# One scatter of whole rows per tile, two under way within an expert, in the routed experts of the second layer

## The chip, the cores and the metric

The kernel runs on one NeuronCore of one Trainium2 chip. The metric is the device time of one launch in microseconds, here the median of three runs. The core has a tensor engine (PE, with its weight loads shown apart as PEld), a vector engine (DVE), a scalar engine (ACT), GpSimd (POOL) and a sync engine (SP), and sixteen DMA engines that all of these feed.

## The reference, cut to what matters

The program computes two layers on `x`, 4 x 512 = 2048 tokens of 512 floats; each layer adds an attention-like block and then a mixture of experts to the residual. The change touches only the very last block, the mixture of experts of the second layer (layer 1):

```python
E, G, TKG, K = (32, 8, 4, 8)
I, SI = (256, 512)
...
_, top_k_index = jax.lax.top_k(masked, K)
tkw = jnp.take_along_axis(scores, top_k_index, axis=-1)
...
flat_idx = top_k_index.reshape(-1)
sort_idx = jnp.argsort(flat_idx)
xs = jnp.repeat(x, K, axis=0)[sort_idx]
group_sizes = jnp.bincount(flat_idx, length=E).astype(jnp.int32)
gate = jax.lax.ragged_dot(xs, w_gate, group_sizes)
up = jax.lax.ragged_dot(xs, w_up, group_sizes)
down = jax.lax.ragged_dot(jax.nn.silu(gate) * up, w_down, group_sizes)
unsort = jnp.argsort(sort_idx)
routed = (down[unsort].reshape(T, K, H) * tkw[..., None]).sum(axis=1)
shared = jax.nn.silu(x @ sw_gate) * (x @ sw_up) @ sw_down
return (routed + shared).reshape(hidden_states.shape)
```

Each of the 2048 tokens goes to 8 different experts of 32. Each expert is a gated two-matmul block with inner width 256, and the eight weighted results of a token are summed onto its row.

## The kernel before, in words

The program runs stage after stage. The last two matter here. The router stage of layer 1 (lines 700 to 1240) computes the shared expert, picks the experts of each token, and writes the token rows, sorted by expert, into a buffer `slots_in` of 128-row tiles. Each expert's rows are padded up to a multiple of 128, so that a tile belongs to one expert; `NTILE1` = 159 tiles are always worked, the last ones being padding alone. The same stage writes the residual with the shared expert's result into the output `out`, and zeros into 128 spare rows behind it (line 838). A list `expert` says which expert each tile has.

The last stage is `expert_stage1` (line 1775). It adds every tile's result to the output rows of its tokens. Tile `t` passes through the engines like this:

- ACT loads rows of four tiles at a time (`load_rows`, L1898) into `xs`, and their records, that is, weights, slot numbers and token number, into `rec` (L1903).
- DVE transposes the rows in `turned_rows` (L1950), and PE multiplies with gate and up weights in `up` (L2012). ACT takes the SiLU (L1886), DVE the product (L1960).
- PE transposes the hidden values (L2019), DVE copies them out (L1955), and PE multiplies with the down weights in `down` (L2028), one tile behind `up`. PE reads the expert of a tile from `ids` with `value_load` (L2005, L2023).
- ACT scales the result by the routing weight and puts it into one of eight buffers `yo` (`empty`, L1893). It waits there for `added`, which says that the scatter of the tile eight before is done with the buffer.
- DVE works out the addresses in `addressed` (L1969 to L1978). It waits for `added` in the same way. A padding row gets a spare row as its address.
- POOL scatters the tile onto the output with an accumulating indirect DMA (`add`, L1865). The output is viewed as half rows of 256 floats, so each tile takes two scatters of 128 half rows. Each half column has a semaphore of its own (`half_out`), and the scatter of a half waits until the same half of the tile before has landed, because two tiles of different experts may hold the same token. So at most two scatters are under way, the two halves of about one tile, and tiles follow each other strictly.

SP refills the ring of four experts' weights (`refill`, L1839 to L1843), each time that `down` has passed the last tile of an expert. `hold` is a wait with a small semaphore increment behind it (L73 and L74). The loop on POOL is unrolled by eight tiles (`OUT`), and the first and last turns are written out. No planner sets the order; each engine runs its list, and semaphores join them.

Of the kernel before, what the change touches and what calls it, by code (L numbers as in the profile page):

```python
# [14 lines left out]
F32 = mybir.dt.float32  # L15
BF16 = mybir.dt.bfloat16
I32 = mybir.dt.int32
ALU = mybir.AluOpType
# [3 lines left out]
P = 128  # L22
B, S, H = 4, 512, 512
T = B * S
NT = T // P
# [13 lines left out]
F1, FS1, K1 = 256, 512, 8  # L39
# [3 lines left out]
NTILE1 = (T * K1 + E * (P - 1)) // P  # L43
# [651 lines left out]
def route_stage(nc, c, I, D, x, L, route, ahead=None, out=None):  # L695
# [10 lines left out]
    with ExitStack() as ctx:  # L706
        pl = Pools(nc, ctx)
# [11 lines left out]
        h = sb("h", [P, FC, S])  # L719
# [11 lines left out]
        else:  # L731
# [4 lines left out]
            base = sb("base", [P, E])  # L736
# [11 lines left out]
        token_i = sb("token_i", [P, NT], I32)  # L748
# [38 lines left out]
        with nc.Block() as block:  # L787

            @block.sync
            def _(sp):  # L790
# [44 lines left out]
                    sp.wait_ge(sem["xout"], 1 + 16 * B)  # L835
                    sp.wait_ge(sem["ahead"], 1 + 16 * loads[0])
                else:
                    sp.dma_start(out[T:T + P, :].rearrange("p (a z) -> p a z", z=P), bc(c["zeros"][:, :], 1, H // P))\
                      .then_inc(sem["xout"], 16)
                    sp.wait_ge(sem["eid"], 1 + 1)  # L840
                    sp.dma_start(D["expert"].rearrange("(p a) o -> p (a o)", a=2), tei[:, :]).then_inc(sem["eidout"], 16)
                    for e in range(AHEAD):
# [4 lines left out]
                                     x[:, b * TB:(b + 1) * TB, :]).then_inc(sem["xout"], 16)  # L847
                    sp.wait_ge(sem["eidout"], 1 + 16)
                    sp.wait_ge(sem["ahead"], 1 + 48 * AHEAD)
                    sp.wait_ge(sem["xout"], 1 + 16 * (B + 1))  # L850

            @block.gpsimd
            def _(pool):
                pool.memset(seg[:, :, :], 1.0).then_inc(sem["ones"], 1)
                pool.memset(seg_t[:, :, :], 1.0).then_inc(sem["ones"], 1)
                if L == 1:
                    pool.memset(seg8[:, :, :], 1.0).then_inc(sem["ones"], 1)
                pool.wait_ge(sem["ones"], 1 + 2 + L)
                pool.memset(seg[:, :, 0], 0.0).then_inc(sem["seg"], 1)
                pool.memset(seg_t[:, :, 0], 0.0).then_inc(sem["seg"], 1)  # L860
                if L == 1:
                    pool.memset(seg8[:, :, 0], 0.0).then_inc(sem["seg"], 1)
                each = 1 if L == 0 else 2
                pool.iota(token_i[:, :], [[each * P, NT]], base=1, channel_multiplier=each).then_inc(sem["iota"], 1)
                for b in range(B if L == 0 else 0):
                    pool.wait_ge(sem["ve"], 1 + b + 1)
                    pool.tensor_tensor(rs[:, b % 2, :], ve[:, b % 2, :], c["minus_half"][:, 0:TB], ALU.pow).then_inc(sem["rs"], 1)

                for t in range(NT):
                    if L == 1 and t < TB:  # L870
                        pool.wait_ge(sem["idx0"], 1 + t + 1)
                    else:
                        pool.wait_ge(sem["idx"], 1 + t // TB + 1 - L)
                    for k in range(K):
# [900 lines left out]
def expert_stage1(nc, c, I, D, x, ends, W, out):  # L1775
# [3 lines left out]
    with ExitStack() as ctx:  # L1779
        pl = Pools(nc, ctx)  # L1780
# [3 lines left out]
        OUT = 2 * RING  # L1784
# [15 lines left out]
        ids = pl.sb("e1_ids", [1, NTILE1], I32)  # L1800
        slot_i = pl.sb("e1_sloti", [P, NTILE1], I32)
        slot1 = pl.sb("e1_slot1", [P, NTILE1])
        spare_i = pl.sb("e1_sparei", [P, 1], I32)
        spare1 = pl.sb("e1_spare1", [P, 1])
        mine = pl.sb("e1_mine", [P, 2, K1])
        wrow = pl.sb("e1_wrow", [P, OUT, 1])
        pad = pl.sb("e1_pad", [P, 2, 1])
        dest = pl.sb("e1_dest", [P, OUT, 2], I32)
        HC = H // 2
        halves = out.rearrange("t (a h) -> (t a) h", a=2)  # L1810
        ps_g = pl.ps("e1_psg", [P, 2, 512])
        ps_h = pl.ps("e1_psh", [P, 2, 512])
        ps_o = pl.ps("e1_pso", [P, 2, 512])
        sem = {n: pl.sem("e1_" + n) for n in ("ids", "w0", "w1", "w2", "w3", "ready", "xsT", "gu", "sg", "h",
                                              "htr", "hT", "down", "yo", "added", "preset", "iota", "named", "chosen", "first", "dest")}
        landed = [sem[f"w{s}"] for s in range(RING)]
        rows_in = [pl.sem0(f"e1_rows{r}") for r in range(2)]
        rec_in = [pl.sem0(f"e1_rec{r}") for r in range(2)]
        half_out = [pl.sem0(f"e1_out{a}") for a in range(2)]
        ROUNDS = -(-NTILE1 // RING)  # L1820
        LAST = NTILE1 - (ROUNDS - 1) * RING
        assert 1 < LAST < RING
# [5 lines left out]
        with nc.Block() as block:  # L1828
# [24 lines left out]
            @block.gpsimd  # L1853
            def _(pool):
                pool.iota(slot_i[:, :], [[P, NTILE1]], base=1, channel_multiplier=1).then_inc(sem["iota"], 1)
                pool.iota(spare_i[:, :], [[1, 1]], base=2 * T + 1, channel_multiplier=2).then_inc(sem["iota"], 1)

                def add(t, q, first=False):
                    hold(pool, sem["yo"], 1 + t + 1, c["held"])
                    for a in range(2):  # L1860
                        if not first:
                            hold(pool, half_out[a], 16 * t, c["held"])
                            if a == 1:
                                pool.sem_inc(sem["added"], 1)  # L1864
                        pool.indirect_dma_start(halves, bass.IndirectOffsetOnAxis(dest[:, q, a:a + 1], 0),  # L1865
                                                yo[:, q, a * HC:(a + 1) * HC], None,
                                                bounds_check=2 * (T + P) - 1, oob_is_err=True, compute_op=ALU.add)\
                            .then_inc(half_out[a], 16)

                add(0, 0, first=True)  # L1870
                for q in range(1, OUT):
                    add(q, q)
                with pool.Fori(1, TURNS - 1) as i:  # L1873
                    for q in range(OUT):
                        add(i * OUT + q, q)
                for t in range((TURNS - 1) * OUT, NTILE1):
                    add(t, t % OUT)
                for a in range(2):
                    pool.wait_ge(half_out[a], 16 * NTILE1)

            @block.scalar
            def _(act):
# [60 lines left out]
            def _(dve):  # L1943
# [18 lines left out]
                def addressed(t, q, n):  # L1962
                    row = rec[:, q // RING, q % RING, :]
                    if q % RING == 0:
                        dve.wait_ge(rec_in[q // RING], 16 * n)
                    if not (isinstance(t, int) and t < OUT):
                        dve.wait_ge(sem["yo"], 1 + t - OUT + 1)
                        dve.wait_ge(sem["added"], 1 + t - OUT + 1)
                    dve.scalar_tensor_tensor(out=mine[:, q % 2, :], in0=row[:, K1:2 * K1], scalar=slot1[:, bass.ds(t, 1)],  # L1969
                                             in1=row[:, 0:K1], op0=ALU.is_equal, op1=ALU.mult).then_inc(sem["named"], 1)  # L1970
                    dve.scalar_tensor_tensor(out=pad[:, q % 2, :], in0=row[:, 2 * K1:RECW], scalar=0.0, in1=spare1[:, :],
                                             op0=ALU.is_equal, op1=ALU.mult).then_inc(sem["named"], 1)
                    dve.wait_ge(sem["named"], 1 + 2 * (t + 1))
                    dve.tensor_reduce(wrow[:, q, :], mine[:, q % 2, :], AX_X, ALU.add).then_inc(sem["chosen"], 1)
                    dve.scalar_tensor_tensor(out=dest[:, q, 0:1], in0=pad[:, q % 2, :], scalar=-1.0, in1=row[:, 2 * K1:RECW],
                                             op0=ALU.add, op1=ALU.add).then_inc(sem["first"], 1)
                    dve.wait_ge(sem["first"], 1 + t + 1)
                    dve.tensor_tensor(dest[:, q, 1:2], pad[:, q % 2, :], row[:, 2 * K1:RECW], ALU.add)\  # L1978
                       .then_inc(sem["dest"], 1)

                def a_round(i, first=False, last=False):
                    for q in range(REST if last else OUT):
# [5 lines left out]
                        product(t, q)  # L1988
                        addressed(t, q, i + 1)

                dve.wait_ge(sem["iota"], 1 + 2)
                dve.tensor_copy(slot1[:, :], slot_i[:, :]).then_inc(sem["preset"], 1)
                dve.tensor_copy(spare1[:, :], spare_i[:, :]).then_inc(sem["preset"], 1)
                dve.wait_ge(sem["preset"], 1 + 2)
                turned_rows(0, 0, 1, first=True)
                a_round(0, first=True)
# [1135 lines left out]
```

## Time and profile before

| | |
|---|---|
| median of three runs | 3114.5 us |
| the three runs | 3119.78, 3114.5, 3114.5 us |
| time of the profiled execution | 3106.26 us |
| its span on the core | 3104.5 us |
| mean granted TensorE clock | 0.949 |
| PE busy | 2687.9 us (87%) |
| DVE busy | 1493.2 us (48%) |
| POOL busy | 1367.1 us (44%) |
| ACT busy | 773.7 us (25%) |
| last stage, first load to end of span | 2155.0 to 3104.5 us |

Times in the rows are counted from the start of the span. Busy shares are averages over stages of different kind. In the last stage the scatters are short instructions on POOL whose transfers run on after them, so a busy share of POOL says little about how far behind the scatters are: that is read from the start times of single instructions.

### The profile page before, as it was taken

The page shows a single profiled execution, that of the slowest core. Times are in us where ns is not written, and L with a number is a line of the kernel's source. Part 1 is how long each engine was busy: PE and PEld are TensorE (multiplying, and loading weights), DVE is VectorE, ACT ScalarE, POOL GpSimd, SP SyncE. Part 2 cuts the span into 40 slices and gives each one's busy share as a digit, 9 for nine tenths or more (in the row PEclk, how much of TensorE's full clock was granted, in tenths as well). Part 3 has the DMA queues.
Part 4 walks back from the last instruction along what each step waited for, and adds up shares of the span by engine and source line. Part 5 has one row for each costly group of instructions (what it writes and reads, how often), then busy time and mean ns, then how long its engine had stood idle before and what let it go on. Part 6 is the DMA issues. An engine that isn't in the chain of part 4 may idle for free. (4 is left out here: it accounts for less than half of the span.)

```text
span 3104.5 us, 33211 instructions
## 1 busy us (share of the span) xinstructions
PE 2687.9 (87%) x8933; PEld 1175.3 (38%) x8936; DVE 1493.2 (48%) x2766; ACT 773.7 (25%) x1190; POOL 1367.1 (44%) x960
## 2 busy tenths in 40 slices
PE   5888975799999887689999998981999999899995
PEld 2343431344444333233333334430444444444442
DVE  7999999332000232266666646310444444344442
ACT  4746653200000010133434332000121111111111
POOL 2777656143000131136646431465455555455555
PEclk8999999999999998889999999995999999999997
DMA  3334222310300599750474001555777776877664
GB/s 125 113 100 111 78 66 54 113 56 14 114 0 14 209 355 333 220 151 1 122 202 116 1 1 59 207 196 194 152 150 161 145 124 126 189 143 163 127 102 53
DMA packets 386408, 385.06 MB, mean 124 GB/s; under 512 B 72195, under 2 KB 311364, under 8 KB 386307
## 3 DMA queue, kind: packets, MB, share of 16 engines
q1 hardware_dynamic: 212434, 243.23, 25.0%
q0 software_dynamic: 68272, 97.19, 16.1%
q10 hardware_dynamic: 105600, 43.35, 6.6%
q8 instruction: 56, 0.92, 0.1%
q14 instruction: 46, 0.37, 0.0%
HBM read 236.15 MB, written 160.27 MB: 128 GB/s over the span
## 5 line engine op out<-in xcount | busy, mean ns | idle before, releaser
L1865 POOL DMA_INDIRECT out_x<-e_yo,e_dest x318 | 493.3, 1551 | 447.8 <-DMA out_x<-e_yo,e_dest 303.5
L2012 PE MATMUL e_psg<-e_wgu,e_xsT 128*128 x1272 | 578.3, 598 | 79.9 <-DVE e_xsT L1950 79.9
L285 POOL TENSOR_TENSOR hc<-hs,bcst 128x1024 f32<-128x1024 f32 x128 | 300.8, 2350 | 175.4 <-DVE ps_b L505 169.5
L2012 PEld LDWEIGHTS e_psg<-e_wgu,e_xsT 128*128 128x128 f32 x1272 | 233.1, 193 | 312.4 <-issue 312.4
L2028 PE MATMUL e_pso<-e_wd,e_hT 128*128 x636 | 306.2, 604 | 27.4 <-DVE e_hT L1955 26.7
L630 PE MATMUL ps_y<-hc,ident 128*128 128x512 f32 x512 | 242.5, 612 | 86.6 <-POOL hc L285 86.4
L511 DVE TENSOR_TENSOR_SCAN hs<-dA,ps_b 128x1024 f32<-128x1024 f32 x128 | 292.6, 2286 | 6.6 <-ACT dA L415 2.4
L1960 DVE TENSOR_TENSOR e_h<-e_psg,e_sg 128x256 f32<-128x256 f32 x159 | 67.3, 423 | 345.1 <-ACT e_sg L1886 335.3
L1233 PE MATMUL r_ps_t<-r_wd,r_h 128*128 128x512 f32 x480 | 209.6, 597 | 8.7 <-DVE r_h L982 5.1
L1886 ACT ACTIVATE e_sg<-e_psg 128x256 f32<-128x256 f32 x159 | 61.1, 384 | 543.9 <-PE e_psg L2012 538.5
L982 DVE TENSOR_TENSOR r_h<-r_ps_u,r_sg 128x512 f32<-128x512 f32 x60 | 41.4, 691 | 319.5 <-PE r_ps_u L1214 296.1
L415 ACT ACTIVATE dA<-dt,a_neg 128x511 f32<-128x511 f32 x256 | 165.4, 713 | 109.2 <-DVE hs L511 104.2
L2028 PEld LDWEIGHTS e_pso<-e_wd,e_hT 128*128 128x128 f32 x636 | 119.3, 191 | 188.5 <-issue 188.4
L2616 DVE TENSOR_REDUCE a_nm<-a_ps 128x2 f32<-128x992 f32 x128 | 146.1, 1185 | 88.9 <-PE a_ps L2860 88.5
L880 POOL DMA_INDIRECT slots_in<-r_xn,scat x128 | 126.6, 989 | 135.8 <-DMA slots_in<-r_xn,scat 60.3
L1893 ACT ACTIVATE e_yo<-e_pso,e_wrow 128x512 f32<-128x512 f32 x159 | 109.3, 687 | 288.4 <-PE e_pso L2028 217.4
L1950 DVE STREAM_TRANSPOSE e_xsT<-e_xs 128x512 f32<-128x512 f32 x159 | 174.6, 1098 | 12.8 <-DMA e_xs<-slots_in 7.3
L630 PEld LDWEIGHTS ps_y<-hc,ident 128*128 128x128 f32 x512 | 93.2, 192 | 230.7 <-POOL hc L285 135.7
L2378 ACT ACTIVATE a_pt<-a_ps 128x1024 f32<-128x1024 f32 (+1 forms) x128 | 126.2, 1022 | 184.0 <-PE a_ps L2877 123.3
L915 ACT ACTIVATE r_sg<-r_ps_g 128x512 f32<-128x512 f32 x60 | 35.8, 597 | 523.2 <-PE r_ps_g L1214 504.4
L505 DVE TENSOR_TENSOR ps_b<-du,bcst 128x1024 f32<-128x1024 f32 x128 | 159.3, 1244 | 8.3 <-DVE hs L511 0.5
L1214 PE MATMUL r_ps_g<-r_xnT,r_wgu 128*128 128x512 f32 x352 | 158.7, 593 | 0.0
(411 smaller groups left out, 3517.8 us busy)
## 6 DMA issues: line engine op xcount, KB each, us to landing
slots_in<-zeros SPq DMA_DIRECT2D x160, 256.0 KB, 2.3
e_xs<-slots_in ACTq DMA_DIRECT2D x160, 256.0 KB
bcst<-bc_rows SPq DMA_DIRECT2D x128, 256.0 KB, 4.3
e_wgu<-in_wg SPq DMA_DIRECT2D x32, 512.0 KB
e_wgu<-in_wu SPq DMA_DIRECT2D x32, 512.0 KB
e_wd<-in_wd SPq DMA_DIRECT2D x32, 512.0 KB
e_w<-in_wg SPq DMA_DIRECT2D x11, 1408.0 KB
e_w<-in_wu SPq DMA_DIRECT2D x11, 1408.0 KB
```

The lines of the kernel that those rows point to most:

```text
L285: pool.tensor_tensor(hc[:, it % 2, half(h), :], hs[:, it % 2, half(h), :], bc(bcst[:, q, 1, :], 1, HB), ALU.mult).then_inc(sem["hc"], 1)
L415: i = act.activation(dA[:, it % 2, t, 1:], dt[:, b % 2, t, 1:], ACT.Exp, scale=a_neg[:, n, t:t + 1])
L505: dve.tensor_tensor(ps_b[:, :, :], du[:, b % 2, half(h), :], bc(bcst[:, q, 0, :], 1, HB), ALU.mult)\
L511: dve.tensor_tensor_scan(hs[:, it % 2, half(h), :].rearrange(flat), dA[:, it % 2, half(h), :].rearrange(flat), ps_b[:, :, :].rearrange(fla ...
L630: i = pe.matmul(ps_y[:, t, :], c["ident"][:, :], hc[:, it % 2, t, :], start=False, stop=False, skip_group_check=True)
L1214: i = pe.matmul(ps[:, f % 2, :], w[:, k, f * P:(f + 1) * P], xnT[:, b, k, :], start=k == 0, stop=k == KH - 1)
L1233: i = pe.matmul(ps_t[:, j % 2, :], h[:, f, j * P:(j + 1) * P], wd[:, f, :], start=f == 0, stop=f == FC - 1)
L1865: pool.indirect_dma_start(halves, bass.IndirectOffsetOnAxis(dest[:, q, a:a + 1], 0), yo[:, q, a * HC:(a + 1) * HC], None, bounds_check=2 * ...
L1950: dve.transpose(xsT[:, q % 2, :, :].rearrange("p k (s j) -> p k s j", j=DQ), xs[:, q // RING % 2, part, :].rearrange("p s (i k) -> p k s i ...
L2012: j = pe.matmul(ps_g[:, q % 2, :], xsT[:, q % 2, k, :], wgu[:, bass.ds(e % RING, 1), k, :], start=k == 0, stop=k == KH - 1)
L2028: j = pe.matmul(ps_o[:, q % 2, :], hT[:, q % 2, a, :], wd[:, bass.ds(e % RING, 1), a, :], start=a == 0, stop=a == NW - 1)
L2616: dve.tensor_reduce(nm[:, i % 8, 2 * z:2 * z + 2], ps[:, at:at + 2, 0:S2], AX_X, ALU.max, negate=True)\
```

## The change

The view of the output as half rows goes. Each tile is scattered with one instruction of 128 whole rows of 512 floats, 2 KB each. Semaphores now go by the parity of the tile (`out_of[0]` for even tiles, `out_of[1]` for odd ones). The scatter of tile `t` always waits for the one of tile `t - 2`. It waits for the one of tile `t - 1` only if that tile has another expert; tiles of one expert share no token, except padding, and padding rows now go to one of two sets of 128 spare rows by parity. Which count of the other parity to wait for stands in a small table `after`, worked out once by DVE from `ids`; POOL reads its entry with `value_load` before each scatter, except for the first three tiles. `added` is now raised when POOL comes to tile `t + 2` and no longer at `t + 1`. DVE loses one small operation per tile (L1978) and the wait ahead of it. The output has 256 spare rows instead of 128, so the router stage writes zeros with two transfers.

```diff
-                    sp.dma_start(out[T:T + P, :].rearrange("p (a z) -> p a z", z=P), bc(c["zeros"][:, :], 1, H // P))\
-                      .then_inc(sem["xout"], 16)
+                    for a in range(2):
+                        sp.dma_start(out[T + a * P:T + (a + 1) * P, :].rearrange("p (a z) -> p a z", z=P),
+                                     bc(c["zeros"][:, :], 1, H // P)).then_inc(sem["xout"], 16)
...
-                each = 1 if L == 0 else 2
-                pool.iota(token_i[:, :], [[each * P, NT]], base=1, channel_multiplier=each).then_inc(sem["iota"], 1)
+                pool.iota(token_i[:, :], [[P, NT]], base=1, channel_multiplier=1).then_inc(sem["iota"], 1)
...
-                pool.iota(spare_i[:, :], [[1, 1]], base=2 * T + 1, channel_multiplier=2).then_inc(sem["iota"], 1)
-
-                def add(t, q, first=False):
+                pool.iota(spare_i[:, :], [[P, 2]], base=T + 1, channel_multiplier=1).then_inc(sem["iota"], 1)
+                pool.iota(after_i[:, :], [[16, (NTILE1 + 1) // 2], [16, 2]], base=-16, channel_multiplier=0).then_inc(sem["iota"], 1)
+                pool.wait_ge(sem["after"], 1 + 1)
+
+                def add(t, q, turn):
+
+                    same = 8 * OUT * turn + 16 * (q // 2)
+                    head = isinstance(turn, int) and turn == 0
                     hold(pool, sem["yo"], 1 + t + 1, c["held"])
-                    for a in range(2):
-                        if not first:
-                            hold(pool, half_out[a], 16 * t, c["held"])
-                            if a == 1:
-                                pool.sem_inc(sem["added"], 1)
-                        pool.indirect_dma_start(halves, bass.IndirectOffsetOnAxis(dest[:, q, a:a + 1], 0),
-                                                yo[:, q, a * HC:(a + 1) * HC], None,
-                                                bounds_check=2 * (T + P) - 1, oob_is_err=True, compute_op=ALU.add)\
-                            .then_inc(half_out[a], 16)
+                    if head and q < 3:
+                        before = 16 if q > 0 else None
+                    else:
+                        before = pool.value_load(after[0:1, bass.ds(t, 1)], min_val=16, max_val=16 * NTILE1)
+                    if before is not None:
+                        hold(pool, out_of[1 - q % 2], before, c["held"])
+                    if not (head and q < 2):
+                        hold(pool, out_of[q % 2], same, c["held"])
+                        pool.sem_inc(sem["added"], 1)
+                    pool.indirect_dma_start(out[:, :], bass.IndirectOffsetOnAxis(dest[:, q, 0:1], 0), yo[:, q, :], None,
+                                            bounds_check=T + 2 * P - 1, oob_is_err=True, compute_op=ALU.add)\
+                        .then_inc(out_of[q % 2], 16)
...
                     dve.scalar_tensor_tensor(out=dest[:, q, 0:1], in0=pad[:, q % 2, :], scalar=-1.0, in1=row[:, 2 * K1:RECW],
-                                             op0=ALU.add, op1=ALU.add).then_inc(sem["first"], 1)
-                    dve.wait_ge(sem["first"], 1 + t + 1)
-                    dve.tensor_tensor(dest[:, q, 1:2], pad[:, q % 2, :], row[:, 2 * K1:RECW], ALU.add)\
-                       .then_inc(sem["dest"], 1)
+                                             op0=ALU.add, op1=ALU.add).then_inc(sem["dest"], 1)
...
+                dve.wait_ge(sem["ids"], 1 + 16)
+                dve.tensor_tensor(apart[:, 1:], ids[:, 1:], ids[:, 0:NTILE1 - 1], ALU.not_equal).then_inc(sem["apart"], 1)
+                dve.wait_ge(sem["apart"], 1 + 1)
+                dve.scalar_tensor_tensor(out=after[:, 1:], in0=apart[:, 1:], scalar=16.0, in1=after_i[:, 1:NTILE1],
+                                         op0=ALU.mult, op1=ALU.add).then_inc(sem["after"], 1)
```

## Rows read from the trace of the kernel before

**Rows 1.** The page: tenths busy per slice; the chain that ended last.
```profile
PE   5888975799999887689999998981999999899995
POOL 2777656143000131136646431465455555455555
PEclk8999999999999998889999999995999999999997
DMA out_x<-e_yo,e_dest 20%; PE e_psg L2012 3%; PE e_pso L2028 1%; POOL out_x L1865 1%; DMA e_xs<-slots_in 0%; POOLq L73 0%; PE e_psh L2019 0%; POOLq L1865 0%; POOLq L74 0%; ACT e_yo L1893 0%; DVE e_xsT L1950 0%; POOLq L1864 0%; ACTq L1898 0%; POOLq L1873 0%; DVE e_hT L1955 0%
```
**Rows 2.** Timeline, ACT's L1893: start, duration, instruction, idle time before and its releaser.
```profile
2177.39 0.69 ACT L1893 ACTIVATE e_yo<-e_pso,e_wrow 128x512 f32<-128x512 f32 x1 [1.33 <-PE e_pso L2028]
2424.77 0.69 ACT L1893 ACTIVATE e_yo<-e_pso,e_wrow 128x512 f32<-128x512 f32 x1 [1.33 <-PE e_pso L2028]
2440.15 0.69 ACT L1893 ACTIVATE e_yo<-e_pso,e_wrow 128x512 f32<-128x512 f32 x1 [5.82 <-DVE e_dest L1978]
3065.75 0.69 ACT L1893 ACTIVATE e_yo<-e_pso,e_wrow 128x512 f32<-128x512 f32 x1 [1.33 <-PE e_pso L2028]
3068.62 0.69 ACT L1893 ACTIVATE e_yo<-e_pso,e_wrow 128x512 f32<-128x512 f32 x1 [2.18 <-PE e_pso L2028]
```
**Rows 3.** Timeline, POOL's L1865.
```profile
2178.99 1.62 POOL L1865 DMA_INDIRECT out_x<-e_yo,e_dest  x1 [23.64 <-ACT e_yo L1893]
3087.97 1.55 POOL L1865 DMA_INDIRECT out_x<-e_yo,e_dest  x1 [0.86 <-DMA out_x<-e_yo,e_dest]
3092.57 1.55 POOL L1865 DMA_INDIRECT out_x<-e_yo,e_dest  x1 [0.93 <-DMA out_x<-e_yo,e_dest]
3094.84 1.55 POOL L1865 DMA_INDIRECT out_x<-e_yo,e_dest  x1 [0.72 <-issue]
```
**Rows 4.** Two stretches: length, busy time of each engine, granted clock, DMA share.
```profile
2177.39:2424.77 247.38, 247.38 (x646) 115.65 (x645) 108.86 (x363) 49.30 (x93) 125.71 (x81) 1.00 0.77 158
2424.77:3065.75 640.98, 611.83 (x1556) 279.75 (x1554) 272.65 (x892) 118.93 (x222) 346.61 (x224) 0.99 0.71 134
```
**Rows 5.** Waits from 1750 us on: in total, times, longest.
```profile
POOL out_x L1865 <- DMA out_x<-e_yo,e_dest: 303.5, 148, 5.7
DVE e_mine L1969 <- POOLq L1864: 138.8, 74, 4.9
PE e_pso L2028 <- DVE e_hT L1955: 26.7, 19, 2.7
```
**Rows 6.** The chain, two stretches: start, duration, what.
```profile
2696.95 8.40 DMA out_x<-e_yo,e_dest
...
3087.97 3.75 DMA out_x<-e_yo,e_dest
...
3091.85 0.72 issue
```
**Rows 7.** The end of the stage (line 1828): duration in ns, first and last start.
```profile
L1828 POOLq DRAIN  x1: 4842/4842/4842, 3098.8 to 3098.8; - x1
```
**Rows 8.** Layer 0's scatter of whole rows (line 1437): ns min/median/max; landing.
```profile
L1437 POOL DMA_INDIRECT x_after<-e_yo,e_dest x16: 1534/1556/2469, 1073.3 to 1271.7; - x16
DMA to landing us min/median/max: 4.9/8.6/10.2
```
**Rows 9.** DMA queue of POOL, 3070 to 3097 us (12 issues): packets, MB, share.
```profile
q0 software_dynamic: 1611, 1.46, 49.3%
```
**Rows 10.** DMA queues of POOL and SP, 1070 to 1280 us.
```profile
q1 hardware_dynamic: 19213, 59.87, 82.3%
q0 software_dynamic: 2304, 4.20, 11.5%
```
**Rows 11.** PE's queue at line 2023: ns min/median/max.
```profile
L2023 PEldq FUSED_REGOPS  x197: 46/151/156, 2172.6 to 3065.3; - x197
L2023 PEldq TENSOR_LOAD <-e_ids x159: 296/302/825, 2172.3 to 3064.9; - x159
```
**Rows 12.** Groups of instructions: busy us, mean ns, idle before.
```profile
L1978 DVE TENSOR_TENSOR e_dest<-e_pad,e_rec 128x1 int32<-128x1 f32 x159 | 28.7, 181 | 5.5
```
**Rows 13.** Timeline of the stage's start.
```profile
2154.97 0.31 SPq L1832 DMA_DIRECT2D e_ids<-tile_expert  x1
...
2155.38 0.24 DVE L1992 CAST e_slot<-e_sloti 128x159 f32<-128x159 int32 x1 [65.94 <-POOL e_sparei L1856]
...
2162.96 2.05 DVE L1950 STREAM_TRANSPOSE e_xsT<-e_xs 128x512 f32<-128x512 f32 x2 [7.28 <-DMA e_xs<-slots_in]
```
**Rows 14.** Waits of SP from 2170 us on.
```profile
SPq L74 <- PE e_pso L2028: 554.2, 25, 48.4
SPq L74 <- DMA e_wd<-in_wd: 5.4, 1, 5.4
```

More of the change, by code:

```diff
@@ L849, in _ @@
                     sp.wait_ge(sem["ahead"], 1 + 48 * AHEAD)
-                    sp.wait_ge(sem["xout"], 1 + 16 * (B + 1))
+                    sp.wait_ge(sem["xout"], 1 + 16 * (B + 2))
             @block.gpsimd
@@ L1802, in expert_stage1 @@
         slot1 = pl.sb("e1_slot1", [P, NTILE1])
-        spare_i = pl.sb("e1_sparei", [P, 1], I32)
-        spare1 = pl.sb("e1_spare1", [P, 1])
+        spare_i = pl.sb("e1_sparei", [P, 2], I32)
+        spare1 = pl.sb("e1_spare1", [P, 2])
+        apart = pl.sb("e1_apart", [1, NTILE1], I32)
+        after_i = pl.sb("e1_afteri", [1, NTILE1 + 1], I32)
+        after = pl.sb("e1_after", [1, NTILE1], I32)
         mine = pl.sb("e1_mine", [P, 2, K1])
@@ L1807, in expert_stage1 @@
         pad = pl.sb("e1_pad", [P, 2, 1])
-        dest = pl.sb("e1_dest", [P, OUT, 2], I32)
-        HC = H // 2
-        halves = out.rearrange("t (a h) -> (t a) h", a=2)
+        dest = pl.sb("e1_dest", [P, OUT, 1], I32)
         ps_g = pl.ps("e1_psg", [P, 2, 512])
@@ L1814, in expert_stage1 @@
         sem = {n: pl.sem("e1_" + n) for n in ("ids", "w0", "w1", "w2", "w3", "ready", "xsT", "gu", "sg", "h",
-                                              "htr", "hT", "down", "yo", "added", "preset", "iota", "named", "chosen", "first", "dest")}
+                                              "htr", "hT", "down", "yo", "added", "preset", "iota", "named", "chosen", "dest",
+                                              "apart", "after")}
         landed = [sem[f"w{s}"] for s in range(RING)]
@@ L1818, in expert_stage1 @@
         rec_in = [pl.sem0(f"e1_rec{r}") for r in range(2)]
-        half_out = [pl.sem0(f"e1_out{a}") for a in range(2)]
+        out_of = [pl.sem0(f"e1_out{lane}") for lane in range(2)]
+        assert NTILE1 % 2 == 1 and OUT % 2 == 0
         ROUNDS = -(-NTILE1 // RING)
@@ L1870, in _ @@
-                add(0, 0, first=True)
-                for q in range(1, OUT):
-                    add(q, q)
+                pool.iota(spare_i[:, :], [[P, 2]], base=T + 1, channel_multiplier=1).then_inc(sem["iota"], 1)
[4 more added lines that the diff above has]
+                    head = isinstance(turn, int) and turn == 0
+                    hold(pool, sem["yo"], 1 + t + 1, c["held"])
+                    if head and q < 3:
[10 more added lines that the diff above has]
+                        .then_inc(out_of[q % 2], 16)
@@ L1873, in _ @@
+                for q in range(OUT):
+                    add(q, q, 0)
                 with pool.Fori(1, TURNS - 1) as i:
                     for q in range(OUT):
[L1875 to L1879, printed above, removed]
+                        add(i * OUT + q, q, i)
+                for q in range(REST):
+                    add((TURNS - 1) * OUT + q, q, TURNS - 1)
@@ L1881, in _ @@
+                pool.wait_ge(out_of[0], 16 * (NTILE1 // 2 + 1))
+                pool.wait_ge(out_of[1], 16 * (NTILE1 // 2))
             @block.scalar
@@ L1970, in addressed @@
                                              in1=row[:, 0:K1], op0=ALU.is_equal, op1=ALU.mult).then_inc(sem["named"], 1)
-                    dve.scalar_tensor_tensor(out=pad[:, q % 2, :], in0=row[:, 2 * K1:RECW], scalar=0.0, in1=spare1[:, :],
-                                             op0=ALU.is_equal, op1=ALU.mult).then_inc(sem["named"], 1)
+                    dve.scalar_tensor_tensor(out=pad[:, q % 2, :], in0=row[:, 2 * K1:RECW], scalar=0.0,
+                                             in1=spare1[:, q % 2:q % 2 + 1], op0=ALU.is_equal, op1=ALU.mult)\
+                       .then_inc(sem["named"], 1)
                     dve.wait_ge(sem["named"], 1 + 2 * (t + 1))
@@ L1989, in a_round @@
                         addressed(t, q, i + 1)
-                dve.wait_ge(sem["iota"], 1 + 2)
+                dve.wait_ge(sem["iota"], 1 + 3)
                 dve.tensor_copy(slot1[:, :], slot_i[:, :]).then_inc(sem["preset"], 1)
                 dve.tensor_copy(spare1[:, :], spare_i[:, :]).then_inc(sem["preset"], 1)
+                dve.wait_ge(sem["ids"], 1 + 16)
[3 more added lines that the diff above has]
+                                         op0=ALU.mult, op1=ALU.add).then_inc(sem["after"], 1)
                 dve.wait_ge(sem["preset"], 1 + 2)
@@ L3127 @@
          for k, v in host.items()}
-    out = nc.dram_tensor("out_x", (T + P, H), F32, kind="ExternalOutput").ap()
+    out = nc.dram_tensor("out_x", (T + 2 * P, H), F32, kind="ExternalOutput").ap()
     program(nc, I, out)
```

## The prediction

> **What bounds the kernel now.** I began with the slices of the page [rows 1]. From about the 28th slice on PE is near full and POOL half busy, which looks like a stage that PE bounds. The chain of waits of the same page says otherwise: what ended last is one run of scatter transfers, 20% of the span, with PE hardly in it. So I looked at when each tile is put into its `yo` buffer by ACT and when POOL scatters it, tile by tile in the timeline.
>
> Tile 0 goes into its buffer at 2177.39 us, tile 46 at 2424.77, tile 157 at 3065.75, the last one at 3068.62 [rows 2]. The first 46 steps take 247.38 us, 5.378 us each, and PE is busy without a gap and at full clock in them [rows 4]. The 111 steps from tile 46 to 157 take 640.98 us, 5.775 each. In this stretch PE has 29.2 us of idle time (640.98 less 611.83), and a clock of 0.99. What holds it back is in the waits [rows 5]: PE waits for DVE's copy, 26.7 us, but DVE itself sits in the address operation until POOL raises `added`, 138.8 us over 74 times. Tile 48, for instance, enters its buffer only after ACT has waited 5.82 us for an address [rows 2]. The eight buffers are full from there on, and PE runs at POOL's pace.
>
> POOL issues the first scatter at 2178.99 us, 1.6 us after the buffer began to be filled, and the last tile's at 3092.57 and 3094.84 [rows 3]. That is 158 tiles in 913.6 us, 5.78 us per tile, and POOL never catches up: at the end it is 24 to 26 us behind ACT. Its idle time is spent on its own transfers, 303.5 us [rows 5]. Calm, a tile takes 4.60 us (3087.97 to 3092.57) [rows 3], for two instructions of 1.55 us and their overhead. A half lands 3.75 us after its issue when it is calm and up to 8.40 us after it under load [rows 6]. So the bound of the stage is the order of the scatters, in two forms: PE's lost pace and the tail.
>
> **The change part by part.** Terms that lie on the path:
>
> 1. PE's lost pace. If POOL keeps up, the 111 steps go at 5.378 us: 596.9 instead of 641.0, a gain of 44.1 us. 29.2 of it is the idle time shown; the rest is the lower clock and slower steps behind each gap. The first stretch is good evidence that nothing else is next in line, since loads of rows and weights and all scatters went on in it, with a DMA share of 0.77 against 0.71 later [rows 4]. SP waited for weights once, for 5.4 us, and otherwise for PE [rows 14], so weights are ahead.
>
> 2. The tail. Today the last issue is 26.2 us behind ACT (3094.84 less 3068.62) [rows 2, 3]. If POOL keeps up it is 1.6 us plus the new read of `after`. PE does such a read in 0.30 us, with 0.15 us of register work behind it [rows 11]. That makes 2.1 us: a gain of 24.1 us.
>
> 3. The last landing. Twelve half scatters took 49.3% of sixteen engines for 27 us, 1.11 us of all engines each [rows 9]. The sixteen whole-row scatters of layer 0 took 11.5% of 210 us, 1.51 us each [rows 10]. So a whole row costs 0.4 us more per landing (and 0.7 us less than two halves). The only whole-row landings in the trace took 4.9 us at best [rows 8], 1.15 more than 3.75. I take 0.8, between the two. The 5.9 us from the last landing (3094.84 + 3.75) to the end of the span, with the drain of 4.84 us in it [rows 7], stay.
>
> Whether POOL keeps up is the real question. Its own time per tile: one instruction, 1.556 us for whole rows in layer 0 [rows 8], so as long as a half's; 0.72 us ahead of it [rows 6]; 0.45 for the read; the waits, some 0.4. That is 3.1 us, against 5.378 that PE leaves. Bounds for the read are nothing (if it runs ahead under the instruction before) and 0.98 us (the longest load of rows 11 and its register work); both stay under. Then the landings. The mean step of today's chain, landing and what follows it to the next issue, is 5.78 us, since POOL is nearly always behind; with 0.4 us more it is 6.2. In an expert of five tiles, tiles 1, 3 and 5 each wait for a landing, and 2 and 4 go beside them. The next expert waits for tile 5. Three steps for five tiles is 3.7 us per tile, and an expert of four takes two steps and 3.1 us, 3.9 per tile. There are 32 experts, so at most 31 changes in 158 neighbours, and the mean is five tiles. At a change POOL falls 6.2 less 5.4, 0.8 us, behind and makes it up on the next tile. Under load one landing may be 9 us; the buffers hold that. `added` comes a tile later than before, which leaves six or seven useful buffers instead of seven or eight; that costs nothing while POOL is one or two tiles behind, and about 5 us of cover if it is not. I add 2 us for some lag left at the end.
>
> Edits at no cost: DVE loses an operation of 0.18 us per tile [rows 12], but PE is full in the first stretch with it, so it gives nothing. The table `after` needs `ids`, loaded from 2154.97 on; DVE idles for 7.28 us until the first rows have landed at 2162.96 [rows 13], which covers a wait for `ids`, two small operations and the third iota. If `ids` came after the rows, some 0.5 us would go. The second transfer of zeros is issued early in the router stage and ends long before the stage does; its cover gone, it would cost a microsecond. The wait for `after` on POOL has nothing behind it until 2178.99 [rows 3].
>
> The sum: 44.1 + 24.1 - 0.8 - 2 = 65.4 us. From 3106.3 (span 3104.5 and 1.8 around it) the profiled execution comes to 3040.9. The median of the runs is 8.2 us above the profiled execution, so the time is 3114.5 - 65.4 = 3049 us.
>
> Two rules weighed. The trace shows 0.3 us for a register read on PE's queue [rows 11]. By the Trainium skill, DMA: Bandwidth & Descriptors, Latency and other measured facts, such a load has a floor of about 600 ns; by it the sum would be 0.3 us less, since only the last tile's read is bare. The trace disagrees for PE, and none of its rows shows a read on POOL. The calm halves landed after 3.75 us [rows 6], with 1.55 us of instruction in it. The same page, Anatomy of one DMA, puts a transfer at 2.0 us fixed and bytes over 436 GB/s, an estimate of 0.3 us more for 256 KB than for 128; the engine time of accumulating rows here gives 0.4, and by the rule the sum would be larger by 0.5 us.
>
> **The rivals.** A, the forecast: POOL keeps up, 3049 us.
>
> B, the landing grows. The one place with whole-row scatters had landings of 8.6 us in the median [rows 8]. With a step of 9.5 us, three steps for five tiles are 5.7 us per tile: 158 tiles end at 2179 + 901 = 3080, then a landing of 4.6 and 5.9 us of end, 3090.5, a gain of 14 us: 3100. For it: two transfers of 256 KB are in flight now. Against it: there SP's queue took 82.3% of the DMA engines [rows 10], while the whole share here is 0.71 to 0.77 [rows 4] with gaps in it, and the scatters' part of that shrinks.
>
> C, slower: pairs don't overlap. If the waits let only one whole-row scatter go at a time, or the second transfer queues behind the first until it has landed, the step of 6.2 us holds for every tile. POOL then issues the last one at 2179 + 158 x 6.2 = 3158.6, and the span ends at 3169, 64.6 us later than now: 3179. It decides from a mean pace of 5.79 us per tile on, where the gain is gone. Against it: halves of one tile overlap on the same queue today, as two issues 2.27 us apart at the end with landings of 3.75 show [rows 3, 6].
>
> D, only the tail goes. If another wait held PE as much in the second stretch, 24.1 - 2.8 = 21 us are won: 3093. The gapless first 46 tiles speak against it.
>
> **How the numbers follow.** A 0.80, with an own range of 3040 to 3062 (the profiled run's offset of 8 us, a lag of up to 10 us). B 0.08, D 0.06, C 0.06. The range reaches towards B and D: 3038 to 3082. What a measurement here can tell from no change is about 0.2%, 6 us; the three runs spread by 5.3. A, most of B and D are faster: 0.91. Same takes 0.03, from between B and C, slower 0.06.
>
> **What would show it.** ACT's L1893 should step at 5.38 us to the end, with the last at 3025 us, and DVE's wait for `added` should be gone. PE should have no gap over 0.3 us in the stage and a clock of 1.00. 159 scatters of about 1.56 us, the last issued 2 to 6 us after ACT's last start. Landings of 4.2 to 9 us. POOL's idle time should be put down to ACT, not to its DMA. The forecast is wrong if POOL is over four tiles behind for long (B), if no scatter is issued while another of its expert is under way (C), or if PE has gaps with another releaser (D).

## The result, and the profile after

The changed kernel takes 3040.64 us in the median of four runs (3035.01 to 3042.43), against 3114.69 us for four runs of the kernel before (3114.5 to 3119.78). The ratio is 0.9764, with a 95% interval of 0.9744 to 0.9784. The forecast was 3049 us and a gain of 65 us; by the medians the gain is 74 us. The profiled executions are 3106.26 and 3042.43 us, with spans of 3104.5 and 3040.7 us, so between them it is 63.8 us.

The page of the changed kernel answers to [rows 1]: first two lines of its slices (tenths busy), then the start of its chain (shares of the span by engine, then by line).

```profile
PE   5888975799999887588999998994499999999998
POOL 2777656233100041126555632257322222232222
...
PE 27%; DMA 1%; issue 0%; POOL 0%; SPq 0%; DVE 0%; ACTq 0%; POOLq 0%; ACT 0%; DVEq 0%
PE e_psg L2025 17%; PE e_pso L2041 9%; PE e_psh L2032 1%; DMA out_x<-e_yo,e_dest 1%; DMA e_xs<-slots_in 0%; POOL out_x L1877 0%; ACTq L1908 0%; SPq L1769 0%; DVE e_xsT L1960 0%; POOLq L1871 0%; ACT e_yo L1903 0%; SPq L1771 0%; DVE e_h L1970 0%; ACT e_sg L1896 0%; POOLq L74 0%
```

The chain has changed hands. Before, scatter transfers held 20% of the span; now PE's matmuls hold 27% and the scatters 1%. POOL's share in the last stage is halved, and PE has no slice below full after the first of the stage, but for the last, in which the span ends.

The timeline of ACT, filling the buffers (start, duration, instruction, idle time before it with its releaser), for tiles 0, 46, 157 and 158:

```profile
2179.00 0.69 ACT L1903 ACTIVATE e_yo<-e_pso,e_wrow 128x512 f32<-128x512 f32 x1 [1.33 <-PE e_pso L2041]
2426.38 0.69 ACT L1903 ACTIVATE e_yo<-e_pso,e_wrow 128x512 f32<-128x512 f32 x1 [1.33 <-PE e_pso L2041]
3025.96 0.69 ACT L1903 ACTIVATE e_yo<-e_pso,e_wrow 128x512 f32<-128x512 f32 x1 [1.33 <-PE e_pso L2041]
3028.83 0.69 ACT L1903 ACTIVATE e_yo<-e_pso,e_wrow 128x512 f32<-128x512 f32 x1 [2.18 <-PE e_pso L2041]
```

The first 46 steps take 247.38 us, to the hundredth what they took before [rows 2]. The next 111 take 599.58 us instead of 640.98, 5.40 us each. The stretches behind this, as in [rows 4]:

```profile
2179.00:2426.38 247.38, 247.38 (x646) 115.65 (x645) 101.50 (x323) 49.30 (x93) 71.43 (x46) 1.00 0.80 163
2426.38:3025.96 599.58, 597.26 (x1556) 279.06 (x1554) 244.84 (x776) 118.87 (x222) 172.11 (x111) 1.00 0.74 143
```

PE is idle for 2.3 us in the second stretch, not 29.2, and its granted clock is 1.00. That is one gap, and the kernel before had it too, with 2.36 us. It is a wait for SP. The chain around it (start, duration, what):

```profile
2845.91 0.58 SPq L1769
2846.54 0.62 SPq L1769
2847.20 0.65 SPq L1771
...
2848.10 0.02 SPq L1839
2848.12 0.48 PE e_psh L2032 x2
```

SP had waited 12.6 us for PE's `down`. Released by it at 2845.84 us, it first issued three loads of a later expert's weights, and only then raised `ready` (L1839), which tells PE that the next expert's weights are there. SP's wait for their landing shows no idle time, so they lay ready. The gap comes from the order of SP's list, not from a late load.

POOL's scatters at the start and the end of the stage, as in [rows 3]:

```profile
2180.59 1.63 POOL L1877 DMA_INDIRECT out_x<-e_yo,e_dest  x1 [23.60 <-ACT e_yo L1903]
2186.68 1.58 POOL L1877 DMA_INDIRECT out_x<-e_yo,e_dest  x1 [4.45 <-ACT e_yo L1903]
2196.91 1.55 POOL L1877 DMA_INDIRECT out_x<-e_yo,e_dest  x1 [8.65 <-issue]
2198.76 1.55 POOL L1877 DMA_INDIRECT out_x<-e_yo,e_dest  x1 [0.30 <-issue]
...
3022.96 1.55 POOL L1877 DMA_INDIRECT out_x<-e_yo,e_dest  x1 [3.84 <-DMA out_x<-e_yo,e_dest]
3028.33 1.57 POOL L1877 DMA_INDIRECT out_x<-e_yo,e_dest  x1 [3.82 <-DMA out_x<-e_yo,e_dest]
3031.20 1.56 POOL L1877 DMA_INDIRECT out_x<-e_yo,e_dest  x1 [1.30 <-issue]
```

The third line is a tile that waited for a landing under load, and the fourth goes out 1.85 us behind it while the third is still under way. The last issue is 2.4 us behind ACT's last start; before, it was 26.2 us.

One row is a trap. The profile puts most of POOL's idle time down to its own transfers, as it did before [rows 5]:

```profile
POOL out_x L1877 <- DMA out_x<-e_yo,e_dest: 343.6, 94, 4.7
POOL out_x L1877 <- issue: 212.6, 57, 9.1
POOL out_x L1877 <- ACT e_yo L1903: 72.9, 8, 23.6
```

Near the end of the stage this is not so. The chain there has landings of 4.75 us, and the issue at 3028.33 us is followed by one at 3031.20, 2.87 us later, with the first still on its way. The 2.87 us is ACT's own step from tile 157 to 158. So POOL waits for ACT there, and the landing only happens to come at about the same time.

### The profile page after: what moved, and what is told of

It is laid out like the page before. It is cut to its first block and busy times, and to the rows that moved or that the text cites. A ratio compares the mean times of both kernels' runs of the same rounds, so it can differ in the third digit from the quotient of the medians.

```text
span 3040.7 us, 33280 instructions
## 1 busy us (share of the span) xinstructions
PE 2672.1 (88%) x8935; PEld 1175.4 (39%) x8936; DVE 1459.8 (48%) x2609; ACT 773.9 (25%) x1190; POOL 1121.2 (37%) x803
## 5 line engine op out<-in xcount | busy, mean ns | idle before, releaser
L1877 POOL DMA_INDIRECT out_x<-e_yo,e_dest x159 | 246.7, 1551 | 629.1 <-DMA out_x<-e_yo,e_dest 343.6
L2041 PE MATMUL e_pso<-e_wd,e_hT 128*128 x636 | 298.9, 592 | 0.7 <-ACT e_yo L1903 0.7
L982 DVE TENSOR_TENSOR r_h<-r_ps_u,r_sg 128x512 f32<-128x512 f32 x60 | 41.4, 691 | 318.1 <-PE r_ps_u L1214 308.8
```

The lines of the kernel that those rows point to most:

```text
L1877: pool.indirect_dma_start(out[:, :], bass.IndirectOffsetOnAxis(dest[:, q, 0:1], 0), yo[:, q, :], None, bounds_check=T + 2 * P - 1, oob_is_ ...
L2041: j = pe.matmul(ps_o[:, q % 2, :], hT[:, q % 2, a, :], wd[:, bass.ds(e % RING, 1), a, :], start=a == 0, stop=a == NW - 1)
```

## The experiments

Every ratio is against the kernel before, which took 3103 to 3122 us beside these runs (medians 3113.2, 3109.5 and 3109.6). The edits are made to the changed kernel, where the text names no other.

**Whole rows alone.** The table `after` is filled as if no neighbour had the same expert.

```diff
-dve.tensor_tensor(apart[:, 1:], ids[:, 1:], ids[:, 0:NTILE1 - 1], ALU.not_equal)
+dve.tensor_tensor(apart[:, 1:], ids[:, 1:], ids[:, 1:], ALU.is_equal)
```

> Whole rows as in the change, but the table is filled as if every tile had another expert than the one before, so each scatter waits for all earlier ones. Order theory (the waits between scatters set the stage): the step of each tile is one whole-row landing, 5.6 us in the mean of the changed kernel's trace, and some 1.0 us to the next issue, 6.6 us; 158 steps put the span's end near 3235 us, slower than before by 60 to 130 us, and POOL is 30 us and more behind ACT. Packet theory (half as many packets and half as many instructions on POOL make the gain, the overlap is a bystander): the time stays near the changed kernel's, below 3070 us.

Measured: 3214.73 us, ratio 1.0337 (1.0312 to 1.0362). Whole rows without the overlap are 102 us slower than the kernel before, inside the 60 to 130 us of the order theory. POOL's first and last issue are at 2178.47 and 3203.18 us, 6.49 us per tile (1024.7 over 158). In the calm end of the stage a tile takes 5.8 us. First the timeline of POOL, then the waits of DVE, which stands for PE's lost pace:

```profile
3191.58 1.55 POOL L1877 DMA_INDIRECT out_x<-e_yo,e_dest  x1 [4.36 <-issue]
3197.41 1.57 POOL L1877 DMA_INDIRECT out_x<-e_yo,e_dest  x1 [4.28 <-issue]
3203.18 1.56 POOL L1877 DMA_INDIRECT out_x<-e_yo,e_dest  x1 [4.20 <-issue]
```

```profile
DVE e_mine L1979 <- POOLq L1876: 447.3, 132, 7.4
```

In the kernel before, the same calm end has 4.60 us per tile with halves [rows 3]. The chain of this run names the landing, 4.88 us for a whole row, where a half took 3.75 [rows 6]:

```profile
3185.67 4.88 DMA out_x<-e_yo,e_dest
```

The packet theory, which expected less than 3070 us, is out.

**The overlap alone.** Two halves per tile as before, four semaphores (parity and half), and the changed kernel's rule.

```diff
-                    if before is not None:
-                        hold(pool, out_of[1 - q % 2], before, c["held"])
...
+                    for a in range(2):
+                        if before is not None:
+                            hold(pool, out_of[1 - q % 2][a], before, c["held"])
+                        if not (head and q < 2):
+                            hold(pool, out_of[q % 2][a], same, c["held"])
+                            if a == 1:
+                                pool.sem_inc(sem["added"], 1)
+                        pool.indirect_dma_start(halves, bass.IndirectOffsetOnAxis(dest[:, q, a:a + 1], 0),
+                                                yo[:, q, a * HC:(a + 1) * HC], None,
```

> Two half-row scatters per tile as before the change, but with the changed kernel's rule: a tile waits for the tile before it only if that one has another expert. Order theory: POOL's two instructions need 4.6 us per tile, under PE's 5.38, and a landing is exposed only at a change of expert, so most of the gain is there: 3045 to 3075 us, with POOL behind at experts of one to three tiles. Packet theory: no gain, 3105 to 3120 us.

Measured: 3043.67 us, ratio 0.9788 (0.9764 to 0.9811). The intervals of this and the changed kernel overlap, so in the timed runs the rule alone brings all that can be measured; the time is 1.3 us below the expected range. The traces show a little more. From ACT's first start to the end of the span it is 865.5 us here and 861.7 in the changed kernel: the last issue is 5.3 us behind ACT's last start and not 2.4, and the rest from there to the end takes 0.9 us more. So 3.8 us of the gain belong to the whole rows, at the very end. POOL is busier than before the change and it doesn't matter (length, busy time of PE, PEld, DVE, ACT and POOL, clock, DMA share, GB/s):

```profile
2200.00:2600.00 400.00, 400.00 (x1043) 187.04 (x1042) 179.81 (x599) 79.90 (x150) 232.83 (x150) 1.00 0.78 152
```

POOL's 150 instructions of this stretch take 232.8 of its 400 us, and PE is full at full clock.

**The read moved ahead of the wait.**

```diff
-                    hold(pool, sem["yo"], 1 + t + 1, c["held"])
                     if head and q < 3:
                         before = 16 if q > 0 else None
                     else:
                         before = pool.value_load(after[0:1, bass.ds(t, 1)], min_val=16, max_val=16 * NTILE1)
+                    hold(pool, sem["yo"], 1 + t + 1, c["held"])
```

> The changed kernel with POOL's read of the table moved ahead of the wait for the tile. Order theory: the read (0.29 us and 0.15 us of register work) is bare in each tile, so the last issue comes about 0.6 us sooner behind ACT (1.8 instead of 2.4 us), the time is the same within what can be measured, and the idle time that the profile puts down to the DMA goes over to ACT. If POOL truly waited for landings within an expert, the distance stays at 2.4 us and the releaser stays the DMA.

Measured: 3040.8 us (3038.13 to 3043.11), the same as the changed kernel. The last issue is at 3028.30 us, 1.8 us behind ACT's last start at 3026.48, 0.6 us closer. The expectation on the releaser was half a miss. The sum put down to the DMA fell from 343.6 to 265.1 us, but it went to "issue" (212.6 to 327.2 us), and in the steady end the profile names the DMA as before:

```profile
3025.43 1.57 POOL L1877 DMA_INDIRECT out_x<-e_yo,e_dest  x1 [3.83 <-DMA out_x<-e_yo,e_dest]
3028.30 1.56 POOL L1877 DMA_INDIRECT out_x<-e_yo,e_dest  x1 [1.30 <-issue]
```

The distance behind ACT fell by 0.55 us, about the read's time (0.29 us and 0.15 of register work), which a true wait for a landing would have swallowed. So the distance decides, and the name of the releaser doesn't.

**Overlap for even tiles only.** Odd tiles always wait for the tile before.

```diff
-                    if head and q < 3:
+                    if q % 2 == 1:
+                        before = 8 * OUT * turn + 16 * (q // 2 + 1)
+                    elif head and q < 3:
```

> The changed kernel with overlap allowed only to even tiles; odd tiles always wait for the tile before them. Order theory with a threshold: two tiles take one landing step and one bare issue, (6.6 + 3) / 2 = 4.8 us per tile, still under 5.38, so the time is the changed kernel's within 8 us. If the gain went with the share of overlapped pairs, the time would lie halfway between the changed kernel's and the serial one's.

Measured: 3039.64 us, ratio 0.9774 (0.9751 to 0.9798), nothing lost. POOL was up to 25.5 us behind ACT in the stretch of small experts, which the eight buffers took. A gain in proportion to the overlapped pairs would have ended halfway to the serial run, near 3128 us, and is out. There is a threshold, and the changed kernel is well inside it.

**Overlap for every fourth tile only.** As the last, with `if q % 2 == 1 or q % 4 == 2:` and `before = 8 * OUT * turn + 16 * ((q + 1) // 2)`.

> Overlap allowed to every fourth tile only, eight buffers. Threshold theory, from the steps measured: 6.49 us for a tile that waits (serial run) and 2.0 for one that goes beside the one before, 31 of 158 of these: 5.61 us per tile, over PE's 5.38, so POOL bounds again, the last issue is at 3062 us, and the time is 3074 us (3062 to 3086). Proportional theory (gain goes with the share of overlapped pairs, 24% of the changed kernel's): 3173 us.

Measured: 3103.25 us, ratio 0.9976 (0.9962 to 0.999). POOL bounds again, as the threshold theory has it, but at 5.80 us per tile (2181.18 to 3097.57), not 5.61; the time is 17 us outside the expected range. The cheap steps were as assumed: 32 of them, 1.94 us each. The waiting ones were not. Worked out from POOL's start times while it was more than 12 us behind ACT, they took 7.09 us in the mean behind an overlapped pair and 6.64 otherwise, where the serial run had 6.49. Timeline of POOL:

```profile
2824.16 1.55 POOL L1879 DMA_INDIRECT out_x<-e_yo,e_dest  x1 [4.24 <-issue]
2826.01 1.55 POOL L1879 DMA_INDIRECT out_x<-e_yo,e_dest  x1 [0.30 <-issue]
2835.41 1.55 POOL L1879 DMA_INDIRECT out_x<-e_yo,e_dest  x1 [7.85 <-issue]
2841.29 1.55 POOL L1879 DMA_INDIRECT out_x<-e_yo,e_dest  x1 [4.33 <-issue]
```

The issue at 2835.41 waited for two scatters. The load of rows and weights is a fixed amount per tile and not per microsecond, so a faster pace meets it in fewer steps and pays more in each. That reading fits; no run isolates it.

**Halves under the same rule.** The "overlap alone" kernel with the last run's condition.

```diff
-                    if head and q < 3:
+                    if q % 2 == 1 or q % 4 == 2:
+                        before = 8 * OUT * turn + 16 * ((q + 1) // 2)
+                    elif head and q < 3:
```

> Two half-row scatters per tile, and overlap allowed to every fourth tile only: the rule of the run with overlap for every fourth tile, on halves. Landing theory: where the waits bound, the row size counts against whole rows, since a calm half lands after 3.75 us and a whole row after 4.75, and the halves of a tile run beside each other. A waiting tile then takes some 0.7 to 1.3 us less than the 6.76 us of that run, the few overlapping ones 1.8 us more, 5.2 to 5.6 us per tile: 3040 to 3075 us, against 3103 for whole rows. Packet theory (fewer, larger packets are worth having in themselves): as slow as whole rows or slower, 3100 us and more.

Measured: 3079.47 us, ratio 0.9907 (0.9885 to 0.9929), 5.61 us per tile. It is 4 us over the range, but 24 us faster than whole rows under the same waits. So where landings bound, whole rows are the worse half of this change; where PE bounds, row size makes no difference.

**Four buffers instead of eight, in the kernel before.**

```diff
-        yo = pl.sb("e1_yo", [P, OUT, H])
+        yo = pl.sb("e1_yo", [P, 4, H])
...
-                    if not first:
-                        act.wait_ge(sem["added"], 1 + t - OUT + 1)
+                    if not (first and t < 4):
+                        act.wait_ge(sem["added"], 1 + t - 4 + 1)
```

> The kernel before with four yo buffers instead of eight. One-chain theory: the chain of scatters alone sets the end, at 5.78 us per tile, and the buffers only decide where the waiting is seen. PE is held back sooner and more (last L1893 near 3082 instead of 3068.6 us) and the tail is shorter (12 to 14 instead of 26 us); the time is the same, 3103 to 3120 us. Two-cost theory (PE's lost pace and the tail are costs of their own that add): PE loses 15 us more and the time goes up by about as much, to 3130.

Measured: 3103.59 us, ratio 0.9986 (0.9973 to 0.9998), the same within the 0.2% that can be told. ACT's last start moved from 3068.62 to 3076.44 us, later by less than expected, though the stage began 1.7 us sooner here (ACT's first start at 2175.70 us). The tail, from ACT's last start to POOL's last issue, shrank from 26.2 to 12.1 us:

```profile
3076.44 0.69 ACT L1893 ACTIVATE e_yo<-e_pso,e_wrow 128x512 f32<-128x512 f32 x1 [2.18 <-PE e_pso L2028]
```

```profile
3088.55 1.55 POOL L1865 DMA_INDIRECT out_x<-e_yo,e_dest  x1 [0.89 <-DMA out_x<-e_yo,e_dest]
```

PE's lost pace and the tail are one cost seen in two places. The chain of scatters has its length (911.3 us here, 915.9 before, first to last issue), and the buffers only share it out. Costs that add would have given 3130 us.

**Four buffers in the changed kernel**, the same edit there.

> The changed kernel with four yo buffers. POOL was at most 8.3 us behind in the changed kernel's trace, and tile t needs POOL to have come to tile t - 2, 10.8 us back: so nothing is lost, 3034 to 3044 us. If the eight buffers carried the gain, PE has gaps again and the time goes up by over 8 us.

Measured: 3043.66 us (3031.96 to 3044.89), ratio 0.9777 (0.975 to 0.9804): nothing lost. POOL was at most 8.3 us behind. Four of the eight buffers, 8 KB per partition, are free for something else.

**Four buffers, overlap for even tiles only.**

> Overlap for even tiles only, and four buffers. With eight buffers POOL fell 25.5 us behind among the small experts and PE lost nothing; four buffers cover some 9 us. Buffer theory: PE loses the difference once, 10 to 17 us, and the time is 3049 to 3057 us. If the distance did not matter, it stays at 3038 to 3042.

Measured: 3051.56 us (3049.11 to 3054.18), ratio 0.9812 (0.9793 to 0.9832), 12 us over the run with eight and inside the range that the buffer theory gave. PE waits again (waits of PE: in total, times, longest):

```profile
PE e_psh L2034 <- DVE e_h L1972: 9.4, 7, 2.5
```

Buffers are worth what POOL falls behind for a while, and only if it can catch up later.

## Why the prediction was right, point by point

**What bounds.** Right, and the four-buffer run shows it better than the argument did: the chain of scatters set the end, in one piece. The split into 44.1 us of lost pace and 24.1 of tail gave the correct sum because both were measured against what PE alone allows. It would mislead anyone who thought that more buffers could win the first term.

**Term 1, PE's pace.** 44.1 us forecast. The 111 steps fell by 41.4 us (640.98 less 599.58). The 2.7 us missing are PE's one wait for SP's `ready`, 2.3 us, and some tenths of slower steps. "Nothing else is next in line" was wrong by that much: the same wait stood in the kernel before at tile 125, inside a stretch that was late anyway. The prediction looked at what SP waits for [rows 14] and took the weights to be ahead. They were, but PE waits for SP's announcement, and that stands in SP's list behind the next three loads. No run moves it.

**Term 2, the tail.** 24.1 us forecast; 26.2 less 2.4 is 23.8. POOL's read of the table takes 0.29 us in the median and 0.15 of register work, as PE's did [rows 11]:

```profile
L1871 POOLq FUSED_REGOPS  x300: 42/147/188, 2197.3 to 3030.0; - x150
L1871 POOLq TENSOR_LOAD <-e_after x156: 284/291/937, 2196.8 to 3029.6; - x156
```

The floor of about 600 ns that the Trainium skill gives for such a load (DMA: Bandwidth & Descriptors, Latency and other measured facts) does not hold on POOL either: half of the reads took 291 ns or less.

**Term 3, the landing.** 0.8 us more was forecast. The calm landing is 4.75 us against 3.75 [rows 6], so 1.0 more:

```profile
3017.57 4.75 DMA out_x<-e_yo,e_dest
```

The 0.4 us of engine time behind the forecast came from two different stages: layer 0's whole rows against this stage's halves [rows 9, 10]. In the calm end of the serial run, from 3150 to 3208 us, ten whole-row scatters give for POOL's queue (packets, MB, share of 16 engines):

```profile
q0 software_dynamic: 1440, 2.62, 37.1%
```

That is 2.15 us of all engines each, against 1.11 for a half [rows 9]: 1.0 more, as much as the landing grew. By the Trainium skill, DMA: Bandwidth & Descriptors, Anatomy of one DMA, a transfer takes 2.0 us and its bytes over 436 GB/s, which makes an estimate of 0.3 us more; for this accumulating scatter the measurement decides, and it is three times that. The end of the span did not come later for it. From the last issue to the end it is 9.5 us now and 9.66 before, since POOL's drain behind the landing [rows 7] is shorter, 3.65 us instead of 4.84. I had it as a constant:

```profile
L1831 POOLq DRAIN  x1: 3654/3654/3654, 3036.2 to 3036.2; - x1
```

**Whether POOL keeps up.** Right in the result. The step of a waiting tile was put at 6.2 us; the serial run has 6.49. POOL's own time per tile was put at 3.1 us; the shortest steps of the trace are 1.85. At a change of expert POOL was to fall 0.8 us behind; at 28 tiles, about as many as there are changes, it falls 1.4 to 5.8 us further behind, and short steps make it up. In the trace POOL is 2 to 4 us behind ACT for most tiles and 8.3 at most. My 2 us for a lag left at the end were not needed.

**The sum against the profiled execution.** 65.4 us forecast, 63.8 found. From ACT's first start to the end of the span it is 927.1 us before and 861.7 after, 65.4; the stages ahead came out 1.6 us longer this time. That is within their spread: in the traces of all eleven kernels ACT's first start lies between 2174.1 and 2181.5 us. The terms of that: 41.4 of PE's pace, 23.8 of the tail, 0.2 of the end. The agreement to the tenth is luck: term 1 was 2.7 us too large, and the 2.8 us taken off for the landing and a lag were not needed.

**The carried offset was mis-sized.** I added the 8.2 us between the profiled execution and the median of three runs to the time after. The changed kernel has no such offset: its profiled execution is 3042.43, its median 3040.64. The kernel before spread from 3103 to 3122 us over the runs of this study, so its profiled 3106.26 was an ordinary draw from the low side, and two of the three shown runs alike at 3114.5 were not a fixed distance. That is nearly the whole difference between 3049 and 3040.6. Its medians beside the later runs, 3109.5 to 3113.2 us, also say that the gain may be nearer 69 to 73 us than 74. Kernels that PE bounds spread too, by 7 us (the changed one) and 13 us (the one with four buffers) in four runs. The traces say where the spread lies, though not what causes it: in the changed kernel and its variants with the read moved, with even tiles only and with four buffers the last stage takes 861.2 to 861.7 us, while it begins anywhere between 2174.1 and 2181.5 us. So the stages ahead spread, and a comparison of the last stage alone is good to half a microsecond for these four.

**The rivals.** B didn't come: steps of 9.5 us and more do occur, but only 7 of the 158 are over 9.5 us and 28 over 7. C, no overlap, is the serial run: 3214.7 us where 3179 was forecast. Its mechanism and side were right and its price, 64.6 us, was low by some 37. The step was 0.29 us too short, which over 158 tiles is 45 us; the offset of 8 us carried in the forecast hides a part. D didn't come.

**What would show it.** The steps (5.40 us in the mean), the clock, the 159 instructions of 1.55 us and DVE's vanished wait for `added` came as written. "No gap over 0.3 us" did not quite: PE has the gap of 2.3 us and one of 0.7. "POOL's idle time should be put down to ACT" did not: the profile names the DMA for 343.6 us, and it took the distance between ACT and POOL, and the run with the read moved, to see that ACT is what it waits for.

**What the change is made of.** The prediction priced both of its parts together. The runs separate them. Overlap alone gives all but 3.8 us of the gain (0.9788 against 0.9764), whole rows alone cost 3.4%, and with both the overlap makes the gain.

## What to carry to other kernels

For a chain of dependent transfers, compare its pace per tile with the pace of the engine beside it: where the chain is slower, it sets the time; where it is faster, only its tail counts, and buffers for the stretches in which it falls behind for a while. Ask first which of the waits protects data (within an expert the wait for the tile before did not), since dropping the others costs nothing, and don't merge transfers that run beside each other while their landing is what is waited for. When a profiled execution and the timed runs differ by a few tenths of a per cent, take the difference as spread and widen the range; don't carry it over as a constant. Where the change touches one stage, compare that stage in the traces.

## What the runs showed of the hardware that was not expected

A scatter that adds 128 rows of 2 KB lands 4.75 us after its issue in the calm end of the stage, and one of 1 KB rows 3.75 us, though POOL's instruction takes 1.55 us for either. Two halves beside each other thus finish a tile at a pace of 4.60 us, and one whole row takes 5.8 us per tile in the serial run. In engine time the whole rows are cheaper all the same. Over 2200 to 3000 us POOL's queue, before and then after the change, shows (packets, MB, share of 16 engines):

```profile
q0 software_dynamic: 39312, 35.80, 35.4%
```

```profile
q0 software_dynamic: 21507, 39.17, 35.4%
```

The same share moves 9% more bytes. These two kernels go at different paces, but the run with the overlap alone goes at the changed kernel's pace and has halves:

```profile
q0 software_dynamic: 42825, 39.01, 38.2%
```

For almost the same bytes its halves take 38.2% where whole rows take 35.4%, 8% more. Less work for the DMA engines and a longer wait for each landing came from one and the same edit.
